# Moving K's last steps, two operand splits and the first output tile of a convolution plus LoRA kernel

## The reference

```python
K = 2 * einsum('hn,hnl->hl', Ct, exp(dtA[:, :, None] * arange(512))).real   # one filter of 512 taps per head
y = irfft(rfft(x, 1024) * rfft(K, 1024))[..., :512] + x * D[:, None]        # causal convolution
x = x + y * (arange(512) < length[:, None])                                 # layer 0
h = einsum('bsd,brd->bsr', x, A[ids]);  lora = einsum('bsr,bor->bso', h, B[ids])
x = x + einsum('bsd,od->bso', x, W) + bias + lora                           # layer 1, W is 512 x 512
```

## Time and profile before

| | us |
|---|---|
| median of 3 runs (lowest, highest) | 216.61 (216.46, 216.75) |
| the profiled execution | 218.4 |
| its span, first to last instruction | 216.4 |
| PE busy in it | 193.1 (89%) |
| DVE busy | 169.8 (78%) |
| ACT busy | 116.1 (54%) |
| POOL busy | 89.9 (42%) |
| mean granted TensorE clock | 0.98 |

### The profile page before, as it was taken

The page is one execution under the profiler, slowest core; times in us unless marked ns, Lnnn a source line. Parts: engine busy times, 40 slices in busy tenths (PEclk is TensorE's granted clock), DMA queues, the critical chain, the costliest instruction groups (busy, mean ns, idle before and its releaser), DMA issues.

```text
span 216.4 us, 4328 instructions
## 1 busy us (share of the span) xinstructions
PE 193.1 (89%) x1046; PEld 167.0 (77%) x1046; DVE 169.8 (78%) x364; ACT 116.1 (54%) x330; POOL 89.9 (42%) x144
## 2 busy tenths in 40 slices
PE   0057999997999999499999999999999999999992
PEld 0045899996999999488888888888888888888881
DVE  3897888679699876479888887878787888878652
ACT  2747362552555234457756566666667575656520
POOL 4840000014347302989535454454545364545500
PEclk9999999999699999979999999999999999999998
DMA  5975999999999999955867777666767667775333
GB/s 142 289 291 157 391 405 407 409 408 410 408 411 407 374 262 323 407 179 178 277 201 218 205 224 200 227 201 214 217 194 228 207 208 211 223 195 185 101 106 133
DMA packets 21520, 56.46 MB, mean 261 GB/s; under 512 B 3394, under 2 KB 3842, under 8 KB 21250
## 3 DMA queue, kind: packets, MB, share of 16 engines
q1 hardware_dynamic: 18370, 47.78, 62.2%
q0 software_dynamic: 2560, 8.39, 13.8%
q10 hardware_dynamic: 576, 0.13, 0.3%
HBM read 45.64 MB, written 10.65 MB: 260 GB/s over the span
## 4 chain that ended last, share of the span: by engine, by line
PE 73%; DMA 7%; DVE 7%; POOL 5%; issue 3%; ACT 2%; SPq 1%; DVEq 0%; ACTq 0%; POOLq 0%
PE y_ps L934 21%; PE k_ps L934 21%; PE z_ps L895 17%; PE z_ps L920 7%; DMA w_sb<-w_t 3%; DMA strip<-k_pad 2%; PE y_ps L943 2%; PE y_ps L944 2%; PE k_ps L943 2%; PE k_ps L944 2%; POOL w_lo L381 2%; DVE z_all L725 1%; DVE xp L719 1%; DVE work L684 1%; DMA tab<-table 1%
## 5 line engine op out<-in xcount | busy, mean ns | idle before, releaser
L895 PE MATMUL z_ps<-xp,strip 128*128 128x512 f32 (+3 forms) x384 | 64.9, 331 | 0.3 <-DMA strip<-k_pad 0.3
L895 PEld LDWEIGHTS z_ps<-xp,strip 128*128 128x128 f32 x384 | 60.6, 200 | 4.5 <-DMA strip<-k_pad 0.4
L406 POOL DMA_INDIRECT b_hl<-b_tab,b_idx x32 | 39.2, 1225 | 10.2 <-issue 9.8
L934 PE MATMUL y_ps<-w_hi,xp 128*128 128x512 f32 x128 | 43.2, 399 | 0.0
L934 PE MATMUL k_ps<-w_hi,xp 128*128 128x512 f32 x128 | 42.6, 393 | 0.0
L401 POOL CAST ag<-a_hl 128x128 fp32r x64 | 23.1, 363 | 41.4 <-PE z_ps L920 30.2
L521 ACT ACTIVATE ag<-a_hl 128x64 fp32r x128 | 25.8, 250 | 22.1 <-issue 22.1
L439 ACT ACTIVATE xp<-z_all 128x512 fp32r<-128x512 f32 x32 | 20.0, 629 | 26.8 <-PE z_ps L895 25.0
L719 DVE TENSOR_TENSOR xp<-z_all,xp 128x512 fp32r<-128x512 f32 x32 | 25.8, 807 | 4.8 <-ACT xp L439 4.5
L934 PEld LDWEIGHTS y_ps<-w_hi,xp 128*128 128x128 f32 x128 | 24.6, 192 | 4.9
L725 DVE TENSOR_TENSOR z_all<-z_ps,mask 128x512 f32<-128x512 f32 (+2 forms) x33 | 22.2, 672 | 7.5 <-PE z_ps L895 7.2
(11 more groups left out here) (116 smaller groups left out, 213.3 us busy)
## 6 DMA issues: line engine op xcount, KB each, us to landing
strip<-k_pad SPq DMA_DIRECT2D x31, 512.0 KB, 8.4
z_all<-x_conv SPq DMA_DIRECT2D x16, 512.0 KB, 9.4
x_t<-x_tile SPq DMA_DIRECT2D x32, 256.0 KB, 2.7
out<-a_raw SPq DMA_DIRECT2D x32, 256.0 KB
a_raw<-a_t SPq DMA_DIRECT2D x2, 512.0 KB, 9.6
x_t<-b_rows SPq DMA_DIRECT2D x2, 512.0 KB, 10.6
w_sb<-w_t SPq DMA_DIRECT2D x2, 512.0 KB, 7.1
b_tab<-b_hl SPq DMA_DIRECT2D x1, 1024.0 KB, 10.6
```

The costliest lines, as they stand in the source:

```text
L406: g.indirect_dma_start(out=b_hl[:, t % BS, :].bitcast(F32), out_offset=None, in_=b_tab, in_offset=bass.IndirectOffsetOnAxis(ap=b_idx[:, t: ...
L895: last = nc.tensor.matmul(z_ps[:, h % ZS, m * P:L], strip[:, h % SS, m * P:(m + 1) * P, t], xp[:, h % XS, 0:LC - m, e, :], start=(n == 0), ...
L934: last = nc.tensor.matmul(y_bank(s), xp[:, s % XS, c, e, :], w[:, c, :], start=(n == 0), stop=False)
```

## The change

- K's steps for group 3 run in iterations 10 to 15 (before 11 to 16); A's quarters are split in iterations 17 to 20 (before 14, 15, 18, 19).
- Group 1's matmuls run after head 0, its store and `k_low` in iteration 4; 15 warming matmuls stand together.
- W's two halves are loaded behind the strips of heads 27 and 29, x's tile 0 behind that of head 30. POOL's order over W is changed.
- Tile 0 starts with the rounded part of x times the rounded part of W, then the remainder of x, then `tile_h`, then W's remainder.
- ACT gathers tile 1's A rows ahead of W's rounding; tile 1's x goes ahead of tile 0's h on ACT and DVE; the wait for the bias moves to the first use of it.

```diff
-A_AT, B_AT = {9: 0, 12: 1}, {16: 0, 18: 1}
-SPLIT_A = {14: 0, 15: 1, 18: 2, 19: 3}
+A_AT, B_AT, W_AT = {9: 0, 12: 1}, {16: 0, 18: 1}, {27: 0, 29: 1}
+XT_AT = 30
+SPLIT_A = {17: 0, 18: 1, 19: 2, 20: 3}
-K_AFTER = {2: 7, 3: 14}
-WARM_0, WARM_1 = 12, 2
-STEPS_AT = {2: (4, 5, 6, 7, 8, 9), 3: (11, 12, 13, 14, 15, 16)}
+K_AFTER = {1: 0, 2: 7, 3: 14}
+WARM = 15
+STEPS_AT = {2: (4, 5, 6, 7, 8, 9), 3: (10, 11, 12, 13, 14, 15)}
@@ SP, in the loop over heads
+                if h == XT_AT:
+                    sp.wait_ge(tab_lo, NW)
+                    load_x_tile(0, 0)
+                if h in W_AT:
+                    load_half(w_sb, w_t, W_AT[h], w_in)
@@ SP, behind the loop
-            sp.wait_ge(tab_lo, NW)
-            load_x_tile(0, 0)
-            for n in range(2):
-                load_half(w_sb, w_t, n, w_in)
             load_x_tile(1, 1)
@@ POOL
-            for c in range(LC):
+            def add_ones(c):
                 pool.wait_ge(w_in[c // 2], 16)
                 d = w_sb[:, c, c * P:(c + 1) * P]
                 g.tensor_tensor(d, d, eye[:, :], ALU.add).then_inc(w_eye, 1)
-                if c % 2:
-                    split_w(c - 1)
-                    split_w(c)
+            add_ones(0)
+            add_ones(1)
+            split_w(0)
+            add_ones(2)
+            add_ones(3)
+            split_w(1)
+            split_w(2)
+            split_w(3)
@@ ACT
             split_x(2)
-            group_store(1)
             split_x(3)
...
             gather(0, 0)
+            gather(1, 1)
             split_w(0)
             split_w(1)
...
-            gather(1, 1)
+            x1_hi(1, 1, True)
             h_down(0, 0)
-            x1_hi(1, 1, True)
             h_rounded(0, 0, True)
@@ DVE
             scale()
-            k_low(1)
             remainder(2)
...
                         dve.wait_ge(tab_lo_stored, 16)
+                        dve.wait_ge(bias_in, 16)
...
-            dve.wait_ge(bias_in, 16)
             dve.wait_ge(z_masked, NH + 1)
             x1_of(1, 1, 0)
+            x1_remainder(1, 1)
             h_masked(0, 0)
-            x1_remainder(1, 1)
@@ PE
-            keep_warm(WARM_0)
-            group(1)
-            keep_warm(WARM_1)
+            keep_warm(WARM)
@@ PE, in tile_base
-                    if first and s == 0 and n % 3 == 0:
-                        pe.wait_ge(w_split, c + 1)
@@ PE, new
+            def first_tile():
+                pe.wait_ge(xhi_early, 1)
+                pe.wait_ge(xhi_done, 1)
+                for c in range(LC):
+                    pe.wait_ge(w_hi_done, c + 1)
+                    nc.tensor.matmul(y_bank(0), xp[:, 0, c, 0, :], w_hi[:, c, :], start=(c == 0), stop=False)
+                pe.wait_ge(xlo_early, 1)
+                pe.wait_ge(xlo_done, 1)
+                for c in range(LC):
+                    nc.tensor.matmul(y_bank(0), xp[:, 0, c, 1, :], w_hi[:, c, :], start=False, stop=False)
+                tile_h(0, 0, True)
+                for c in range(LC):
+                    pe.wait_ge(w_split, c + 1)
+                    last = nc.tensor.matmul(y_bank(0), xp[:, 0, c, 0, :], w_lo[:, c, :], start=False, stop=False)
+                last.then_inc(base_done, 1)
-            pe.wait_ge(xlo_early, 1)
-            tile_h(0, 0, True)
-            tile_base(0, 0, True)
+            first_tile()
```

More of the change, by code:

```diff
@@ L254, in load_strip, with load_x_tile @@
                 sp.dma_start(strip[:, s, j0:j1, :].rearrange("p l e -> p (l e)").bitcast(F32), src).then_inc(done, 16)
+            def load_x_tile(t, s):
+                sp.dma_start(x_t[:, s, :], x_tile[t]).then_inc(xt_landed[s], 16)
             sp.wait_ge(pad_stored, 16)
@@ L276, in _ @@
                     load_half(b_raw, b_rows, B_AT[h], b_in)
-            def load_x_tile(t, s):
-                sp.dma_start(x_t[:, s, :], x_tile[t]).then_inc(xt_landed[s], 16)
+                if h == XT_AT:
[3 more added lines that the diff above has]
+                    load_half(w_sb, w_t, W_AT[h], w_in)
             def store(t, s):
```

## The result

| | before | after |
|---|---|---|
| median (20 executions each) | 216.68 us | 215.86 us |
| lowest, highest | 215.14, 220.10 | 214.99, 216.70 |
| profiled execution | 218.4 | 214.99 |
| its span, mean granted clock | 216.4, 0.98 | 213.2, 1.00 |

After over before is 0.995 (95% interval 0.9929 to 0.9971): about 1 us faster. I had forecast 3.7 less, 212.9, and a range of 211.2 to 215.2. The result lies above the range.

What follows compares the result with a forecast made beforehand. PE was taken as the bound, losing time at group 3's stall, late strips and the change of parts. Convolution -1.9 and tile 0 -1.8 sum to -3.7: profiled 214.7, median 212.9 us, range 211.2 to 215.2.

Steps and rivals of the forecast that it cites:

- The offset between profile and median: Whole kernel: the median lies 1.8 us below the profiled 218.4, a difference taken over unchanged to the forecast.
- a term of 1.64: Head 15, behind group 3's wait: half clock makes it 3.6 us instead of 1.96, a loss expected to go.
- The convolution, minus 1.9: Heads 15 to 20: 3.14 us of stall and half clock go, strip waits return some; head 20 starts 1.9 sooner.
- My own lower bound, 0.3: Convolution term: smallest gain, minus 0.3, if a strip wait brings one half-clock stretch of 1.64.
- Group 1, 0: Group 1 behind head 0: value 0, bounds minus 0.3 to plus 1.64; strips 8 and up land as before.
- The A splits, 0: A's splits in iterations 17 to 20: DVE keeps 1 us of lead, value 0, bounds 0 to plus 3.6.
- DVE becomes the bound: Rival, heads 17 to 24: POOL's pieces hold the mask too, DVE needs 2.68 per head; 217.6 us, chance 0.08.
- Tile 0, minus 1.8: Change of parts: tile 2 starts 9.6 us after the convolution's end instead of 11.4, bounds 8.2 and 11.
- the rival's 8.3: Rival, ports fall kindly: POOL's W pieces lie between DVE's operations, tile 2 8.3 after the convolution; 211.6 us, chance 0.16.
- half clock behind the new waits: Rival: half clock after waits for strips 19, 20 or before tile 0 costs 1.3 in the middle; 214.2 us, chance 0.27.

Runs made afterwards that it cites:

- c1: Kernel before with group 3's steps one head earlier and A's splits three heads later, nothing else; 216.83 us, ratio to before 0.9966.
- g1: Kernel before with group 1's matmuls, store and remainder moved behind head 0 and the 15 warming matmuls; 217.25 us, ratio to before 1.0004.
- n1: Changed kernel with group 1 back ahead of head 0, all else of the change kept; 214.70 us, ratio to before 0.989.
- h1: n1 with strip 8 held on SP's queue until head 4 is convolved, 3 us more; 216.06 us, ratio to before 0.9986.
- c2: c1 with two more pairs of x loaded ahead of the first strip; 218.53 us, ratio to before 1.0063.
- a1: Changed kernel measured once more, unaltered; 215.62 us, ratio to before 0.9925.
- w1: Kernel before with matmuls whose results nobody reads ahead of group 3 (5) and tile 0 (13); 215.79 us, ratio to before 0.9958.
- t1: Changed kernel with group 1, group 3's steps and A's splits as before, so the tile part alone; 215.36 us, ratio to before 0.9912.
- b1: Kernel before measured once more, unaltered; median 216.93 us, its profiled execution 217.01 us at clock 0.992.
- d1: f1 with group 3's steps and A's splits as in the kernel before; 215.93 us, ratio to before 0.9957.
- f1: n1 with one more pair of x ahead of the first strip and A's quarters split in iterations 16 to 19; 214.29 us, ratio to before 0.9889.

## Why the prediction was wrong in size

*The offset between profile and median.* This is the step that failed first: "the median of the runs, 216.61, is 1.8 lower; I take the difference over to it". The 1.8 was no constant. It was mostly the half-clock stretch behind group 3, which I had priced at 1.64: the profiled execution belongs with the 44 of 109 at 218.1, the median with the 58 at 216.7. I had the evidence: a profile 1.8 above the median, and a term of 1.64 that a stretch of clock would explain. The forecast counted that term as a gain of the change in every execution.

*The convolution, minus 1.9.* The mechanism (the DMA queue limits what the stall can give back) was right, and the waits came at heads 19 and 20 as forecast, 0.39 and 0.40 for my 0.6. The size was wrong because the head times of before were. In a typical execution strips already wait, the convolution ends at 87.5, and the steps give 0.1 (c1). My own lower bound, 0.3, belonged to the median.

*Group 1, 0.* Head 1's start was right (23.32 for 23.5), the transfers were not: "the queue still holds 5 us of earlier transfers then, so they land as before". They were issued before it ran dry, and still the rate fell to 264 to 326 GB/s for 4 us. It cost 0.4 to 0.8 (g1, n1) where I had put 0, and h1 shows that a late issue alone brings the same fall and a cost of 1.1 to 1.2 at full clock. Why full DMA engines move less after such a hold stays open: no experiment took the burst apart from the shorter queue.

*The A splits, 0.* Right in the changed kernel, with the wrong lead: the index block takes 4.9 us, not 1.7, as POOL holds three of its six small operations (c2). It is 4.9 in the changed kernel too (59.00 to 63.86), without a wait on PE. The rival "DVE becomes the bound" appeared when the strips stopped waiting (c2), but by these six operations; its own condition, that POOL holds the mask too, is not what c2 shows.

*Tile 0, minus 1.8.* Place by place right: PE starts 1.7 after the convolution (1.5), tile 1 5.7 after (5.8), tile 2 9.5 after (9.6). DVE's small addition took 0.95 and its remainder 0.94 beside POOL's three pieces; in a1 they fell more kindly, 0.19 and 0.40, and tile 2 came 9.1 after, not at the rival's 8.3. But I set a full-clock tile 0 against a half-clock one. Without half clock the kernel before needs 10.0 (w1), not 11.4, so the tile part is worth 0.5 of tile time in the profile of after and 0.9 in a1's. In whole executions it is worth 1.0 at full clock and 1.3 at 0.99 (t1 against before), or 1.2 and 1.5 (n1 against c1, which has one execution at full clock). Of this, 0.2 lies outside the span, which my sum had no term for: every kernel with the tile part has 1.70 to 1.80 us there, every other 1.91 to 2.09. Why stays open. Against a typical execution of before, where tile 0 is at half clock, the profiled execution of after does start tile 2 by 1.8 us sooner (97.38 against 99.19 in b1), but 9 of the first 20 executions of the changed kernel are not at full clock.

*The sum by what was measured*, at full clock: steps 0 to -0.1, tile -1.2, group 1 +0.8, in all -0.4 to -0.5; the classes say 215.8 to 215.4, and at 0.99 they say 216.7 to 216.2. The rest of the median's gain is the mix of classes: 21 of 32 executions of the changed kernel are at full clock (before 7 of 109), and none is in the third class (before 44 of 109). Which part of the change makes the mix better is not taken apart; c1 and t1 each have 2 of 12 in the third class.

*The rival "half clock behind the new waits"* fits 11 of 32 executions of the changed kernel and costs 0.8 there, not 1.3; both of its profiles are at full clock, so where the stretch lies is read only from n1 (0.50 at 90 to 92 us, tile 0). The rule of the Trainium skill ("TensorE: Matmul & The Clock Gate", HAM oscillation) describes a loop whose DMA waits are longer than the matmuls of a pass, and which starts every pass slow. I applied it to much shorter waits, and it does not show here: strip waits of 0.17 to 1.12 us, beside 1.96 us of matmuls per head and at 3 or 4 of 32 heads, leave the clock at 1.00 throughout the convolution (after, a1). No run here has waits as long as a pass, so the rule itself is not tested.

## What to carry to other kernels

Before a sum is made from one profile, see to which class of executions it belongs: if it lies off the median by about the price of one stretch at half clock, that stretch is luck and not part of the gain. The profiled execution can as well be the fastest of its kernel (c2, h1). A stall in front of a saturated queue is worth nothing until the queue is relieved; price it by when the queue delivers, in a typical execution. An issue moved later on an in-order DMA queue costs even while the queue is still full.

## What was not expected of the hardware

- After SP's queue was held 3 us and then issued several transfers in a burst, the DMA engines stayed at share 0.99 to 1.04 but moved 264 to 326 GB/s for 4 us instead of 410 (after, h1). Why stays open.
- GpSimd's operations hold DVE operations with a single SBUF tensor input too: a 128x160 cast of 0.24 us took 1.33. Masks with a PSUM source kept 0.68.
- The same idle stretch on TensorE is followed by 1.2 GHz in some executions and not in others. Before group 3, 1.50 us in the first profile of before was; 1.43 in t1's, 1.49 in d1's and, in the same program, 1.08 in b1's were not. Ahead of tile 0, 1.85 us in n1's and f1's profiles was; 1.86 in h1's was not.
